# The root products of two graph layers in three fp32r terms in place of plain fp32, in a fused kernel of four graph-network blocks on one Trainium2 core

## The reference, cut to what matters

```python
def _rgcn_conv(x, weight, root, bias, src, dst, etype):
    out = x @ root + bias                      # the "root" product: 256x768 @ 768x768
    for r in range(4):
        sel = etype == r
        deg = zeros(n).at[dst].add(sel)
        norm = where(sel, 1.0 / maximum(deg[dst], 1.0), 0.0)
        out = out + segment_sum((x @ weight[r])[src] * norm[:, None], dst, n)
    return out

x = relu(_rgcn_conv(h, W1, root1, b1, ...))    # the kernel's layer 2
x = relu(_rgcn_conv(x, W2, root2, b2, ...))    # layer 3
x =      _rgcn_conv(x, W3, root3, b3, ...)     # layer 4
```

## Time and profile before

| | |
|---|---|
| median of 3 runs | 913.54 us (913.54 to 914.11) |
| the profiled execution | 910.11 us |
| its span, from first to last instruction | 908.3 us |
| mean granted TensorE clock | 0.962 |
| PE / weight loads / DVE / ACT / POOL busy | 89% / 70% / 67% / 42% / 57% |
| the chain that ended last, by engine | PE 56%, POOL 27%, DVE 12%, ACT 3% |
| layer 2 / 3 / 4 on PE (root of tile 0 or first aggregate to last product) | about 522 to 595 / 595 to 675 / 675 to 756 us |

### The profile page before, as it was taken

The page is one execution under the profiler, slowest core; times in us unless marked ns, Lnnn a source line. Parts: engine busy times, 40 slices in busy tenths (PEclk is TensorE's granted clock), DMA queues, the critical chain, the costliest instruction groups (busy, mean ns, idle before and its releaser), DMA issues.

```text
span 908.3 us, 10069 instructions
## 1 busy us (share of the span) xinstructions
PE 812.0 (89%) x3992; PEld 632.4 (70%) x3996; DVE 611.4 (67%) x698; ACT 378.9 (42%) x410; POOL 516.4 (57%) x225
## 2 busy tenths in 40 slices
PE   8999998999788999889887699999999996777887
PEld 3569966775455997766564489979988995644554
DVE  8955068999998306899999666458528755643642
ACT  1125266767652425676746234224433331211321
POOL 0347549999994754999999448518643861000000
PEclk9999999999999999999989799999999998778999
DMA  8046426244331742603522265517535536000000
GB/s 357 1 112 225 150 62 171 70 140 139 105 104 40 259 154 61 172 0 128 174 77 98 86 248 160 202 38 273 177 104 202 180 119 264 1 0 1 1 0 35
DMA packets 24262, 110.98 MB, mean 122 GB/s; under 512 B 3604, under 2 KB 5908, under 8 KB 23832
## 3 DMA queue, kind: packets, MB, share of 16 engines
q1 hardware_dynamic: 23096, 104.24, 35.2%
q10 hardware_dynamic: 1120, 6.10, 1.7%
HBM read 100.63 MB, written 0.79 MB: 112 GB/s over the span
## 4 chain that ended last, share of the span: by engine, by line
PE 56%; POOL 27%; DVE 12%; ACT 3%; issue 2%; DMA 0%; DVEq 0%; ACTq 0%
PE ps L955 21%; POOL prod L561 18%; PE ps L903 9%; POOL prod L564 6%; PE ps L940 6%; DVE prod L1706 5%; PE ps L1334 4%; POOL w_lo L549 3%; PE ps L1010 2%; PE ps L1031 2%; PE ps L1405 2%; PE ps L1188 1%; DVE qi_t L1724 1%; PE ps L1328 1%; PE ps L1310 1%
## 5 line engine op out<-in xcount | busy, mean ns | idle before, releaser
L549 POOL TENSOR_TENSOR w_lo<-w_raw,w_hi 128x1536 fp32r<-128x1536 f32 x54 | 198.2, 3680 | 144.1 <-ACT w_hi L615 144.0
L561 POOL TENSOR_TENSOR prod<-prod 128x1024 f32<-128x1024 f32 x94 | 225.3, 2412 | 40.9 <-DVE prod L1706 40.5
L720 ACT ACTIVATE prod<-ps 128x1024 f32<-128x1024 f32 x192 | 187.8, 1024 | 96.4 <-PE ps L1141 72.1
L1706 DVE TENSOR_TENSOR prod<-prod,ps 128x2048 f32<-128x2048 f32 x96 | 218.7, 2279 | 3.2 <-ACT prod L720 2.5
L1141 PE MATMUL ps<-sel_pair,h_and_q 128*128 128x512 f32 x384 | 130.4, 452 | 22.2 <-ACT prod L720 21.9
L903 PE MATMUL ps<-w_raw,h_t 128*128 128x384 f32 x408 | 142.1, 495 | 0.0
L615 ACT ACTIVATE w_hi<-w_raw 128x1536 fp32r<-128x1536 f32 x54 | 80.3, 1488 | 137.2 <-PE ps L955 93.5
L955 PE MATMUL ps<-w_hi,yt_hi 128*128 128x384 f32 x432 | 111.2, 338 | 5.3 <-POOL w_lo L549 5.2
L903 PEld LDWEIGHTS ps<-w_raw,h_t 128*128 128x128 f32 x408 | 79.0, 196 | 46.2 <-issue 2.9
L955 PE MATMUL ps<-w_lo,yt_hi 128*128 128x384 f32 x432 | 109.9, 335 | 0.0
L955 PE MATMUL ps<-w_hi,yt_lo 128*128 128x384 f32 x432 | 109.9, 335 | 0.0
(11 more groups left out here) (194 smaller groups left out, 1057.4 us busy)
## 6 DMA issues: line engine op xcount, KB each, us to landing
w_raw<-weights SPq DMA_DIRECT2D x105, 768.0 KB, 4.4
wa_in<-weights SPq DMA_DIRECT2D x6, 768.0 KB, 5.9
w_gat<-weights SPq DMA_DIRECT2D x6, 768.0 KB, 7.9
w_query<-weights SPq DMA_DIRECT2D x3, 768.0 KB, 11.1
h_and_q<-stage_hi SPq DMA_DIRECT2D x24, 96.0 KB, 2.1
h_and_q<-stage_lo SPq DMA_DIRECT2D x24, 96.0 KB, 2.2
a_vec<-gat_vectors ACTq DMA_DIRECT2D x1, 2048.0 KB, 8.1
q_t<-queries ACTq DMA_DIRECT2D x1, 1536.0 KB, 12.2
```

What stands on the lines that cost most here:

```text
L549: pool.tensor_tensor(Wl[:, j, :], raw_slab(U, 0, j), Wh[:, j, :], ALU.subtract).then_inc(w_lo_ready, 1)
L561: pool.tensor_tensor(v[:, :, 0:32], v[:, :, 0:32], v[:, :, 32:64], ALU.add).then_inc(folded_once, 1)
L720: act.activation(slot_view(s)[:, :, 32 * u:32 * u + 32], args.rearrange("p b (n l) -> p (b n) l", l=LH), ACT.Sigmoid).then_inc(sigmoid_rea ...
L1706: TT(slot_view(s), slot_view(s), ps[:, 6, o:o + L].unsqueeze(1).broadcast_to([P, NB, L]), ALU.mult).then_inc(products_ready, 1)
```

## The change

The roots of layers 3 and 4 become units that are split like the relations: `SPLIT` now holds their units too, which makes three more slabs in each of the two layers for `w_hi` on ACT and `w_lo` on POOL. `root_part(layer, t, j)` computes one slab of one tile with the same three terms as `product`. Its left operand lies in place 0 of `YTh` and `YTl`: ACT rounds the turned tile there (`root_hi`), and DVE takes the rest (`root_lo`). The order at the border is new on PE, ACT and DVE. `HT2` goes away; layers 0 to 2 keep the fp32 root.

```diff
-SPLIT = [UNIT[l] + v + 1 for l in range(LAYERS) for v in range(RELATIONS[l])]
+SPLIT = [UNIT[l] + v for l in range(LAYERS) for v in range(l < 3, RELATIONS[l] + 1)]
...
+            def root_hi(layer, t):                      # ScalarE
+                act.wait_ge(turned[t], layer + 1 if t == 0 else INPUT[layer] + 1)
+                copy(YTh[:, 0, :, t * P:(t + 1) * P], chunk_tile(4 + 2 * t, KC)).then_inc(root_hi_ready[t], 1)
...
                     relu_out(layer, 0)
-                    keep_turned(layer + 3, layer + 2)
-                    w_hi(UNIT[layer + 1] + 1, (0,))
+                    root_hi(layer + 1, 0)
+                    w_hi(UNIT[layer + 1], (0,))
                     h_hi(layer + 1, 0)
+                    w_hi(UNIT[layer + 1], (1,))
                     relu_out(layer, 1)
                     h_hi(layer + 1, 1)
+                    w_hi(UNIT[layer + 1], (2,))
+                    root_hi(layer + 1, 1)
+                    w_hi(UNIT[layer + 1] + 1, (0,))
...
+            def root_part(layer, t, j):                 # TensorE
+                if j == 0:
+                    pe.wait_ge(root_lo_ready[t], layer - 2)
+                    root_bias(layer, pair(layer, t))
+                pe.wait_ge(w_lo_ready, SPLIT_AT[UNIT[layer], 0, j])
+                mm = three_terms(0, j, t, pair(layer, t), False)
+                if t == 1:
+                    mm.then_inc(w_used, 1)
...
                 if layer > 2:
-                    root(layer, 0, 0, 4)
-                turn(1, e)
-                root(layer, 0, 4, KC)
+                    root_part(layer, 0, 0)
+                    turn(1, e)
+                    root_part(layer, 0, 1)
+                    root_part(layer, 1, 0)
+                    root_part(layer, 0, 2)
...
                 aggregate(layer, 1)
-                root(layer, 1, 4 if degrees is not None else 0, KC)
+                if layer < 3:
+                    root(layer, 1, 4 if degrees is not None else 0, KC)
+                else:
+                    root_part(layer, 1, 1)
+                    root_part(layer, 1, 2)
                 aggregate(layer, 2)
...
+            def root_lo(layer, t):                      # VectorE
+                dve.wait_ge(root_hi_ready[t], layer - 2)
+                cols = slice(t * P, (t + 1) * P)
+                TT(YTl[:, 0, :, cols], chunk_tile(4 + 2 * t, KC), YTh[:, 0, :, cols], ALU.subtract).then_inc(root_lo_ready[t], 1)
...
                 if layer > 2:
+                    root_lo(layer, 0)
                     h_lo(layer, 0)
-                    keep_turned(layer + 2)
                     h_lo(layer, 1)
+                    root_lo(layer, 1)
```

More of the change, by code:

```diff
@@ L260, in build @@
         turn_kept = [sem(f"turn_kept{t}") for t in range(NT)]
+        root_hi_ready = [sem(f"root_hi_ready{t}") for t in range(NT)]
+        root_lo_ready = [sem(f"root_lo_ready{t}") for t in range(NT)]
         half_turned = sem("half_turned")
@@ L604, in _ @@
             for layer in range(2, LAYERS):
-                for v in range(RELATIONS[layer]):
-                    w_lo(UNIT[layer] + 1 + v)
+                for v in range(layer < 3, RELATIONS[layer] + 1):
+                    w_lo(UNIT[layer] + v)
             for n in (2, 3):
@@ L644, in keep_turned @@
                 act.wait_ge(turned[0], nth)
-                copy(turned_h(e)[:, :, 0:P], chunk_tile(4, KC)).then_inc(turn_kept[0], 1)
+                copy(HT[:, :, 0:P], chunk_tile(4, KC)).then_inc(turn_kept[0], 1)
+            def root_hi(layer, t):
+                act.wait_ge(turned[t], layer + 1 if t == 0 else INPUT[layer] + 1)
+                copy(YTh[:, 0, :, t * P:(t + 1) * P], chunk_tile(4 + 2 * t, KC)).then_inc(root_hi_ready[t], 1)
             def h_hi(layer, t):
@@ L910, in turn, with root_bias, three_terms @@
                 ins.then_inc(turned[t], 1)
+            def root_bias(layer, bank):
+                row, slot = ((0, 0), (0, 1), (2, 0), (2, 1), (3, 0))[layer]
+                bias_mm(row, slot, bank)
+            def root_part(layer, t, j):
[6 more added lines that the diff above has]
+                    mm.then_inc(w_used, 1)
+            def three_terms(s, j, t, bank, last):
+                for k in (2 * j, 2 * j + 1):
+                    for n, (Y, Wx) in enumerate(((YTh, Wh), (YTh, Wl), (YTl, Wh))):
+                        for h in range(2):
+                            c0 = (k % 2) * F + h * FH
+                            mm = pe.matmul(ps[:, bank + h, 0:FH], Y[:, s, k, t * P:(t + 1) * P], Wx[:, j, c0:c0 + FH],
+                                           start=False, stop=(last and k == KC - 1 and n == 2))
+                return mm
             def root(layer, t, k0, k1):
@@ L917, in root @@
                     pe.wait_ge(turn_kept[t], e + 1)
-                    row, slot = ((0, 0), (0, 1), (2, 0), (2, 1), (3, 0))[layer]
-                    bias_mm(row, slot, bank)
+                    root_bias(layer, bank)
                 for k in range(k0, k1):
@@ L947, in product @@
                 U = UNIT[layer] + v
-                bank, s = pair(layer, t), v % 2
                 pe.wait_ge(w_lo_ready, SPLIT_AT[U, 0, j])
                 pe.wait_ge(yt_lo_ready, BEFORE[layer] + 3 * (v - 1) + (j + 1))
[L951 to L957, removed]
+                return three_terms(v % 2, j, t, pair(layer, t), last)
             def layer_products(layer, degrees=None):
@@ L962, in layer_products @@
                 if layer > 2:
-                    root(layer, 0, 0, 4)
-                turn(1, e)
-                root(layer, 0, 4, KC)
+                    root_part(layer, 0, 0)
[4 more added lines that the diff above has]
+                else:
+                    turn(1, e)
+                    root(layer, 0, 4, KC)
                 if degrees is not None:
```

9 lines of the change are left out of this document (3 added, 6 removed).

## The result

The changed kernel takes 919.74 us (median of five runs, 918.00 to 922.84) against 913.54 of the kernel before, run beside it (911.99 to 914.33): ratio 1.0075, 95% interval 1.0049 to 1.0100. It is slower by 0.75%, and the whole interval lies above 1; 920.2 was forecast. The profiled execution went from a span of 908.3 to 916.2. In the batch of E5 to E8 one of the 19 runs of the kernel before was slow (1052.94 us at a granted clock of 0.742): the ratios leave it out, and its median, given as 912.79, is 912.29 without it.

The account below looks back on a forecast made before the run. PE was taken to bound these layers, POOL close behind at layer ends. Border 2/3 +0.1 and layer 4 with its border +6.6 gave +6.7 on 910.11: 916.8, median 920.2; 8-in-10 range 913.0 to 925.5.

Parts of the forecast that it names:

- PE's saving and the borders: Borders 2/3 and 3/4: PE saves 2.97 us a layer, waits for POOL of 2.85 eat it, +0.1 each.
- The mark of 1.9 us: Border: rival (b) was to decide if DVE pushed POOL by less than 1.9 us in all.
- rival (b): Border: a waiting DVE instruction does not push POOL's next, each border gains 0.6 to 0.9, time 912.0; chance 0.11.
- SP's loads: Loads come up to 12 us sooner; cost put at nothing, as PE does not wait for them.
- The counts: Layer 4, DVE: six count operations start at 693.2, two held by POOL's w_lo, end at 702.9 instead of 692.27.
- rival (a): Layer 4: the counts slip through or are blocked once, +0 to +3, time 913.5 to 916.5; chance 0.25.
- The attention's operations: Layer 4, DVE: attention_counts meet relation 3's three w_lo, which end at 735.8 if all get in, 732.3 if two.
- The last relation: Layer 4: POOL's w_lo come late for PE, so tile 0 ends 4.9 to 8.4 us later.
- three blocks: Layer 4: all three w_lo get in among the attention's operations; last w_lo end at 746.9, 751.9, 755.4, tile 0 +8.4.
- The sign that I gave: Last relation of layer 4: PE waits on POOL of 3 to 4 us in all three slabs of tile 0.
- Rival (c): Last relation: PE's waits drop its clock to 1.2 GHz, tile 1's pass doubles at worst, +14, 927.5; chance 0.12.
- The 3.4 from the profiled execution to the median: Whole run: median of the runs before lay 3.4 us above the profiled execution; same gap added to 916.8 gave 920.2.

Follow-up runs that it names:

- E5: Changed kernel with the six count operations at the start of layer 2, the first root slab's w_lo on DVE, ACT and DVE reordered at borders: 909.87 against 912.79 before.
- E8: The changed kernel itself, measured again in a later batch against the kernel before: 920.89 against 912.79, ratio 1.0089.
- E4: Changed kernel with the counts at the start of layer 2, and attention_counts and their transposes before layer 2's relation 2: 918.71 against 911.98 of the kernel before.
- E3: Changed kernel with only the six count operations moved, from layer 4 to the start of layer 2: 913.91 against 911.98 of the kernel before, ratio 1.0017.
- E7: Changed kernel, counts left late, attention_counts moved behind layer 4's relation 4 and its logit_weights: 917.93 against 912.79 of the kernel before, ratio 1.0053.
- E6: E5 with the last slab of the last relation of layers 2 to 4 also on DVE: 904.41 against 912.79 of the kernel before, ratio 0.9922.
- E1: The change made for layer 3's root only: 913.66 against 911.98 of the kernel before, ratio 1.0019.
- E2: The change made for layer 4's root only: 919.2 against 911.98 of the kernel before, ratio 1.0095.

## Why the prediction was right

**PE's saving and the borders: right.** 2.97 saved and 2.85 of waits gave +0.1 on paper; it was 0.00 at border 2/3, with waits of 1.32 and 1.11 for the 1.5 and 1.35. E5 shows that the two sides are what they were said to be: take the waits away and 2.34 of the saving comes out. The pushing that I took from the earlier trace rows is there, as POOL's timeline of border 3/4 has three `w_lo` in 11.81 and DVE's two `h_lo` in 7.75:

```profile
673.24 11.81 POOL L546 TENSOR_TENSOR w_lo<-w_raw,w_hi 128x1536 fp32r<-128x1536 f32 x3 [7.45 <-ACT w_hi L612]
673.93 7.75 DVE L1608 TENSOR_TENSOR h_lo<-h,h_hi 128x768 fp32r<-128x768 f32 x2 [1.15 <-ACT h_hi L612]
```

The mark of 1.9 us that I had set for rival (b) was a bad one: the pushing comes to 1.4 (11.81 less three `w_lo` of 3.48), and my own forecast's was 0.8 and 0.85. Rival (b) falls by its mechanism: DVE's waiting `h_lo` did push POOL, slab 1 was done at 680.9, as forecast (681.1), and the border gave nothing.

The layer 3 excess of 0.74 was not foreseen. I had put SP's loads at nothing because PE does not wait for them. DVE does, for `wa_in`, and PE waits for DVE through POOL: 0.3 to 1.2 us in five of the six profiles of the table above that have layer 3's root split.

**The counts: right.** Start 693.2 and end 702.9 were forecast, 692.89 and 702.42 came. Two of them were held, as taken, and rival (a) falls: between chained DVE operations POOL got its turn both times.

The Trainium skill, "SBUF — State Buffer", section "Who interferes with whom", has copy, cast, tensor_scalar in their two-port forms and any DVE operation with two SBUF inputs as the ones that lock out a reading GpSimd and are locked out. The runs agree for each of the four kinds: 3.63 for the copy, 3.45 for the cast in E4, 3.62 for the scalar operation, and two operations of 6.42 for the two-input ones. One place differs from that rule, and there the measurement counts: in the last section, two-input operations of DVE run inside POOL's scalar operations without being held.

**The attention's operations: right in mechanism, at the upper end.** If all three `w_lo` got in, they were to end at 735.8, and if two, at 732.3; all three did, and the end is 734.47. My middle value of the two cases was near it by luck: who gets in was not in the trace of before.

**The last relation: right in mechanism.** `w_lo` were to end at 746.9, 751.9 and 755.4 (three blocks); they ended at about 745.3, 750.2 and 753.6 [PE's rows above, and POOL's 741.03 + 12.57], each 1.6 to 1.8 earlier. The sign that I gave, waits of 3 to 4 us in all three slabs, came only for the first: 3.03, 1.66, and none for the third, because PE was still on slab 1 at half clock. Tile 0's residual is 6.62 late, where 4.9 to 8.4 was said and 6.6 taken. E3 gives the chain of causes: with the counts away, both collisions and the lost head start go together.

**What one term hid.** I treated the late counts as the cause of the attention's collision and that as the only thing that costs. E7 says that 2.96 of 6.79 remain when the second collision is gone (more by the medians), because the late counts also delay the load of `wa_in`. The forecast's sum held because both ways lead to a late `w_lo` in the last relation; the price of the late counts alone was wrong, and so E7 missed its 914 to 916.

**Rival (c): seen, and cheap.** The clock did fall to its 1.2 GHz level behind the wait of 3.03. Slab 1's products took until 753.85 where they would have been done by about 752.4, but slab 2's `w_lo` came only at 753.6: it cost 0.2 on the path, not up to 14. Before the fall PE had stood still for 3.03; the borders' gaps of 1.1 to 1.3 left the clock at 1.00 in the windows I read. It is not cheap everywhere. The clock also fell behind the waits of 2.54 in E4 and E7 and of 3.05 in E6, and there PE had the whole of tile 1 ahead of it. In E4 the windows 590 to 592, 592 to 594 and 594 to 596 have 0.88, 0.50 and 0.77, which is 1.7 us of full-speed work lost (an estimate from these three).

**The time, and what stays open.** 920.2 against 919.74 and, in E8, 920.89. That it is so near is in part luck. The 3.4 from the profiled execution to the median went in as a constant; after the change it was 1.7 (919.74 less 918.00). The profiled execution was 1.2 over the forecast's 916.8, and 1.3 of that is the short tail of the profile of before.

Not settled is how the medians go with the stages. They lose more than layer 4's stage in four kernels with layer 3's root split: 1.7 in E1 against +0.01, 1.9 in E3 against -0.23, 5.1 in E7 against +2.96, 8.1 in E8 against +6.72. In E2, where it is not split, it is 7.2 against +6.77. But the change's own first batch goes the other way, 6.2 against +6.79. Where the medians lose more it is some 1.4 to 2.2 us, of which I forecast 0.1 for layer 3's root, and the late `wa_in` accounts for a mean of 0.5 in the profiles. What the rest is, and why the load takes longer with the split root, no run isolates.

## What to carry to other kernels

Before a cheap piece of PE work is bought with more work on a second engine, find out when that engine is needed and who sits in its holes: here the small DVE operations lived in POOL's idle time, and taking the hole away cost more than the products saved. Sum up what is late behind a collision until something stops waiting, since a collision of 6 us made a second of 9. Work that two engines can do belongs to the one that is idle at the moment it is due, slab by slab: with the counts moved away, the first root slab of two borders and the last slab of three layers on DVE turned +0.8% into -0.9%. Some of this is to be had without the change: the last slabs alone gave -0.4%. And a load that PE never waits for can still cost PE time, if a third engine waits for it and holds off the one that PE needs.

## What the runs showed of the hardware

A POOL operation does not hold DVE off in every form. In the trace of before, POOL's and DVE's timelines:

```profile
44.79 6.50 POOL L573 TENSOR_SCALAR sel_pair<-const_in 64x1024 fp32r<-64x1024 f32 x2
```

```profile
44.87 0.68 DVE L1657 TENSOR_TENSOR rest_count<-a_i 128x512 f32<-128x512 int16 x1
...
46.45 1.40 DVE L1661 TENSOR_TENSOR rest_count<-rest_count,a_i 128x512 f32<-128x512 f32 x2
```

Four of DVE's two-input operations run at their 0.7 each inside POOL's scalar operations, which read a broadcast view (a fifth, L1662 at 48.61, takes 1.49, for a reason that no run shows); against POOL's `w_lo` the same kind takes 3.5. Whether it is the operation or the view of its input that decides, no run here tells.

Two DVE operations that follow each other without a wait can let a queued POOL instruction in between, as L1868's did after the change (DVE's durations in ns, minimum/median/maximum):

```profile
L1868 DVE TENSOR_TENSOR looped<-looped,ident x2: 2883/3247/3611, 724.4 to 727.2; 128x128 f32<-128x128 f32 x2
```

One was held for what was left of one `w_lo`, the other for all of the next; free, both take 0.49 (E3). In layer 4 each `w_lo` in the queue cost DVE one block: two for the counts, three for the attention's operations.
